# Attention scores of batches 1 to 14 from scaled fp16 parts of x2 instead of fp32r parts

## The chip, the cores and the metric

The kernel runs on one core of a Trainium2 chip. Its engines are TensorE (PE in the profile, with its weight loads shown apart as PEld), VectorE (DVE), ScalarE (ACT), GpSimd (POOL) and SyncE (SP, which issues most DMAs). The metric is the device time of one execution in microseconds. Before the change it is 1338.56 us, the median of 3 runs (1338.45 to 1338.69).

## The reference, cut to what matters

Sixteen batches of x, each 512 tokens by 512 features, go through two residual steps. fc1 is 2048 x 512, fc2 384 x 2048, and each batch adds a 128 x 2048 expert that its index picks.

```
h      = gelu(x @ fc1_w.T + fc1_b)                      # 512 x 2048 per batch
x      = x + concat(h @ fc2_w.T + fc2_b, h @ experts_w[i].T + experts_b[i])     # called x2 below
scores = tanh(x @ W1 + b1) @ v                          # W1 is 512 x 128, one score per token
p      = softmax(scores under a prefix, suffix or "not itself" mask)
out    = x + (p @ x) / number of unmasked tokens
```

The change is about `x @ W1`, the product that the tanh reads, in batches 1 to 14.

## The kernel before, in words

Everything lies transposed: features on the 128 partitions, tokens along the free side, so x of a batch is four chunks `chunk(b, c)` of 128 x 512 in `xr`. Each engine has its program written out by hand; there is no scheduler. An engine works its program strictly from first to last, and where it needs another's result it waits on a semaphore (`e.wait_ge`).

The large products run in fp16 in two parts. A value times a power of two is rounded to fp16 (the high part, made by ACT: `hh`, `xh`, `eh`), the rest is taken as fp16 again (the low part, made by DVE: `hl`, `xl`, `el`, line 1176), and three matmuls add high x high, high x low and low x high. fc1 uses seven products per pair of hidden tiles in place of eight: `product1` to `product7` in `cycle`. Between them ACT copies a half bank of PSUM (`copy_first`, `copy_fifth`, line 701) and DVE adds two halves (`add_first`, line 1225, and `add_second`, line 1230). `product7` of a pair waits for that pair's `add_first` (semaphore `added0`).

One batch b goes through these stages on PE. Six cycles of fc1, fc2 for output chunk 0 among the last of them, then fc2 for chunks 1 and 2. In the middle of chunk 1 stands `chain_sum`, a small matmul (line 342) that sums the bounds of batch b+1 over the partitions; DVE turns them into powers of two at once (`batch_scales`, lines 1134 to 1148). fc2 for chunk 3 follows, and then `opening(b)`: the attention products of chunks 0, 1 and 2 (`attend`, lines 484 to 487), the end of fc2 for chunk 3, products 1, 5, 6, 2 of pair 0 and product 1 of pair 1 of batch b+1, `attend(b, 3)`, and right behind it `product7(b+1, 0)`.

The product with W1 is made of three fp32r matmuls per chunk: `awl` x `x2h`, `awh` x `x2h`, `awh` x `x2l`. ACT rounds the chunk to fp32r (`split_x2_high`), DVE subtracts to get the rest (`x2_low`, line 1236). Chunk 3 comes late: ACT evacuates it from PSUM (`evacuate(b, 3)`, line 826) in the opening itself.

DVE does four kinds of work: low parts, the PSUM additions, the scales, and the pooling (scans and products over tokens, lines 1328 to 1454) of the batch before. The pooling is a Python generator, and `pool(n)` puts its next n instructions in at that place, so it fills DVE's time between the pieces that PE waits for. Between `batch_scales(b+1)` and `add_first(b+1, 0)` DVE has in this order: four `combine`, three pool steps, `x2_low(b, 0)`, low parts of x for batch b+1 with pool steps among them, `x2_low(b, 1)`, more of the same, `x2_low(b, 2)` and nine pool steps.

In batch 0 there is a lead-in of its own. DVE makes the masks (`masks`, 13 small instructions on 128 x 16) before the low parts of fc2's third weight chunk.

Of the kernel before, what the change touches and what calls it, by code (L numbers as in the profile page):

```python
# [35 lines left out]
def build(nc, xT, idx, pt, w1, b1, w2, b2, ew, eb, aw, ab, av, iota, ident, tokens, out):  # L36
# [14 lines left out]
    def over(name, shape, at, dt=f32):  # L51
# [18 lines left out]
    x2h_at = (here(), g_at, g_at + 8 * S)  # L70
    x2h = [nc.alloc_sbuf_tensor_at(f"x2h{c}", [P, S], f32r, offset=at) for c, at in enumerate(x2h_at)]
# [9 lines left out]
    awl = [sb("awl0", [P, A], f32r), sb("awl1", [P, A], f32r),  # L81
           nc.alloc_sbuf_tensor_at("awl2", [P, A], f32r, offset=early_at)]
    awh = nc.alloc_sbuf_tensor_at("awh", [P, KD, A], f32r, offset=aws_at)
    x2l_at = (here(), g_at + 4 * S, g_at + 12 * S)
    x2l = [nc.alloc_sbuf_tensor_at(f"x2l{c}", [P, S], f32r, offset=at) for c, at in enumerate(x2l_at)]
# [144 lines left out]
    def sems(name, n):  # L230
# [5 lines left out]
    vcol_in, vmax_done, v_scaled, atth_done, attl_done = (  # L236
        sem(n) for n in ("vcolin", "vmax", "vscaled", "atth", "attl"))
# [96 lines left out]
    def tensor_program(eng):  # L334
# [142 lines left out]
        def attend(b, c):  # L477
# [151 lines left out]
        e.wait_ge(vmax_done, 1)  # L629
        chain_sum(9, hc(1), vc + 1)  # L630
# [65 lines left out]
    def scalar_program(eng):  # L696
# [137 lines left out]

        def split_x2_high(b, c):
            e.wait_ge(x2_done, nth_chunk(b, c))
            if c in (1, 2):
                e.wait_ge(xl_done, nth_x(b + 1, (T1, T3)[c - 1]))
            copy(x2h[c][:, :], chunk(b, c)).then_inc(x2h_done)

        def tanh(b):
# [6 lines left out]
            act(att, pa, ACT.Tanh, bias=abs_[:, 0:1]).then_inc(tanh_done)  # L848
# [122 lines left out]
        for b in range(1, B):  # L971
# [138 lines left out]
    def vector_program(eng):  # L1110
# [39 lines left out]
        def batch_scales(b):  # L1150
            chain_scale(8 + b, hc(b), hc(b) + 3 if b > 1 else vc + 1)
# [754 lines left out]
```

## Time and profile before

| what | value |
|---|---|
| median of 3 runs | 1338.56 us |
| the profiled execution's own time | 1338.24 us |
| its span | 1336.5 us |
| one batch in steady state (rows of one place, batch 5 to 6) | 81.4 us |
| PE busy | 1329.4 us, 99% |
| DVE busy | 1246.9 us, 93% |
| ACT busy | 877.9 us, 66% |
| granted clock of TensorE | full (1.00), the 2.4 GHz level, in every slice |

The span runs from the first to the last instruction; 1.7 us of the execution lie outside it. Matmuls are pipelined: one shows as longer than the distance to the next, so the distance between starts is what it costs PE. DVE and ACT show a similar overlap of some 0.09 us between an instruction and the next.

### The profile page before, as it was taken

What the parts mean: (1) busy time and instruction counts of PE and PEld (TensorE: products, weight loads), DVE (VectorE), ACT (ScalarE), POOL (GpSimd) and SP (SyncE); (2) the same over time, 40 slices, a digit from 0 to 9 for tenths busy, and PEclk for the clock granted to TensorE, in tenths of its full rate; (3) what the DMA queues carried; (4) which work ended last, traced back from release to release, by engine and by line L of the source; (5) the groups of instructions that cost most, each with busy time, mean ns of one, the idle gap of its engine ahead of it and who ended that gap; (6) DMA issues with size and microseconds to landing.
All of it is one profiled execution on the core that took longest, in us unless ns stands there. A gap on an engine that the chain in (4) does not pass through costs nothing.

```text
span 1336.5 us, 21986 instructions
## 1 busy us (share of the span) xinstructions
PE 1329.4 (99%) x8681; PEld 864.5 (65%) x8681; DVE 1246.9 (93%) x2097; ACT 877.9 (66%) x1523; POOL 7.4 (1%) x12
## 2 busy tenths in 40 slices
PE   9999999999999999999999999999999999999998
PEld 4458476584856748567584765847668485674855
DVE  7988899999999999999999999999999999999998
ACT  4868848476593756938478484775847669385762
POOL 0000000000000000000000000000000000000002
PEclk9999999999999999999999999999999999999999
DMA  8410020110201102011020211102011020110006
GB/s 296 145 46 32 1 72 25 48 49 1 79 17 57 39 1 80 16 64 33 8 80 8 66 31 36 60 1 80 17 55 40 1 80 16 64 33 6 33 15 118
DMA packets 30488, 65.13 MB, mean 49 GB/s; under 512 B 6194, under 2 KB 7858, under 8 KB 27954
## 3 DMA queue, kind: packets, MB, share of 16 engines
q1 hardware_dynamic: 28802, 61.11, 14.0%
q0 software_dynamic: 1152, 2.09, 1.2%
q8 instruction: 68, 1.11, 0.4%
q10 hardware_dynamic: 432, 0.53, 0.1%
q14 instruction: 34, 0.28, 0.1%
HBM read 44.86 MB, written 18.87 MB: 48 GB/s over the span
## 4 chain that ended last, share of the span: by engine, by line
PE 99%; DMA 0%; DVE 0%; ACT 0%; issue 0%; DVEq 0%; ACTq 0%
PE ps L458 16%; PE ps L460 16%; PE ps L459 16%; PE ps L377 14%; PE ps L379 14%; PE ps L378 14%; PE ps L348 1%; PE ps L484 1%; PE ps L485 1%; PE ps L487 1%; PE ps L359 1%; PE ps L363 1%; PE ps L361 1%; PE ps L491 0%; DMA xr<-in_xT 0%; PE ps L569 0%
## 5 line engine op out<-in xcount | busy, mean ns | idle before, releaser
L460 PE MATMUL ps<-hl,w2h 128*128 128x512 f16 x768 | 291.1, 379 | 0.0
L458 PE MATMUL ps<-hh,w2l 128*128 128x512 f16 x768 | 291.1, 379 | 0.0
L459 PE MATMUL ps<-hh,w2h 128*128 128x512 f16 x768 | 291.0, 379 | 0.0
L377 PE MATMUL ps<-xh,w1h 128*128 128x256 f16 x960 | 261.7, 273 | 0.0
L378 PE MATMUL ps<-xl,w1h 128*128 128x256 f16 x960 | 261.7, 273 | 0.0
L379 PE MATMUL ps<-xh,w1l 128*128 128x256 f16 x960 | 261.7, 273 | 0.0
L726 ACT ACTIVATE g<-ps,b1s,ds 128x512 f32<-128x512 f32 x240 | 173.4, 773 | 97.6 <-PE ps L379 84.4
L377 PE MATMUL ps<-xh,ch 128*128 128x256 f16 x720 | 196.5, 273 | 0.0
L378 PE MATMUL ps<-xl,ch 128*128 128x256 f16 x720 | 196.3, 273 | 0.0
L379 PE MATMUL ps<-xh,cl 128*128 128x256 f16 x720 | 196.3, 273 | 0.0
L1176 DVE SCALAR_TENSOR_TENSOR hl<-g,ix,hh 128x512 f16<-128x512 f32 x244 | 178.4, 744 | 3.1
L701 ACT ACTIVATE hh<-g,ix 128x512 f16<-128x512 f32 x244 | 162.1, 718 | 0.0
L701 ACT ACTIVATE ps<-ps 128x256 f32<-128x256 f32 x120 | 44.6, 371 | 163.8 <-PE ps L379 163.8
L460 PEld LDWEIGHTS ps<-hl,w2h 128*128 128x128 f16 x768 | 75.1, 98 | 90.6
L458 PEld LDWEIGHTS ps<-hh,w2l 128*128 128x128 f16 x768 | 75.1, 98 | 87.4 <-DVE hl L1176 3.0
L459 PEld LDWEIGHTS ps<-hh,w2h 128*128 128x128 f16 x768 | 75.1, 98 | 82.7 <-issue 0.7
L377 PEld LDWEIGHTS ps<-xh,w1h 128*128 128x128 f16 x960 | 93.9, 98 | 19.0
L378 PEld LDWEIGHTS ps<-xl,w1h 128*128 128x128 f16 x960 | 93.9, 98 | 18.8
L379 PEld LDWEIGHTS ps<-xh,w1l 128*128 128x128 f16 x960 | 93.9, 98 | 10.8
L458 PE MATMUL ps<-hh,el 128*128 128x512 f16 x240 | 91.1, 380 | 0.0
L460 PE MATMUL ps<-hl,eh 128*128 128x512 f16 x240 | 91.0, 379 | 0.0
L459 PE MATMUL ps<-hh,eh 128*128 128x512 f16 x240 | 91.0, 379 | 0.0
(246 smaller groups left out, 2351.2 us busy)
## 6 DMA issues: line engine op xcount, KB each, us to landing
xr<-in_xT SPq DMA_DIRECT2D x62, 256.0 KB, 3.2
er<-in_ew SPq DMA_DIRECT2D x15, 1024.0 KB, 5.5
out<-xr SPq DMA_DIRECT2D x60, 256.0 KB, 2.4
raw<-in_w SPq DMA_DIRECT2D x28, 256.0 KB, 6.0
er<-in_w SPq DMA_DIRECT2D x3, 1024.0 KB, 9.9
out<-sums POOLq DMA_DIRECT2D x8, 255.5 KB, 5.2
xr<-in_ew SPq DMA_DIRECT2D x1, 1024.0 KB, 5.8
out<-xn SPq DMA_DIRECT2D x3, 256.0 KB, 3.2
```

The costliest lines, as they stand in the source:

```text
L348: m = mm(pf[k % 4], w1r[k][:, c * P:(c + 1) * P], xr[:, 0, c, :], start=c == 0, stop=c == KD - 1)
L359: mm(pf[k % 4], w1h[:, k, c, :], xh[:, c, :], start=c == 0, stop=False)
L361: mm(pf[k % 4], w1h[:, k, c, :], xl[:, c, :], start=False, stop=False)
L377: mm(to, wh, mh, start=i in (1, 5) and c == 0, stop=False, skip_group_check=True)
L378: mm(to, wh, ml, start=False, stop=False, skip_group_check=True)
L379: m = mm(to, wl, mh, start=False, stop=c == 1, skip_group_check=True)
L458: mm(po(b, o), wl, hh[:, k, :], start=False, stop=False, skip_group_check=True)
L459: mm(po(b, o), wh, hh[:, k, :], start=False, stop=False, skip_group_check=True)
L460: m = mm(po(b, o), wh, hl[:, k, :], start=False, stop=k == NH - 1, skip_group_check=True)
L701: return act(o, x, ACT.Copy, scale=scale)
L726: act(in_two(g_of(b, k)), src, ACT.Gelu, bias=b1s[:, k:k + 1], scale=ds1[:, b % 2, p:p + 1]).then_inc(gelu_done)
L1176: return stt(o, src, scale, hi, ALU.mult, ALU.subtract)
```

## The change

ACT now first multiplies a chunk by a per-batch scale and writes it as fp32 (`scale_x2` into `x2s`), and then rounds that times 2^-11 to fp16 (`x2h`). DVE's `x2_low` makes the low part from the two as fp16, 2^11 times as large as it would be (`x2l = x2s - 2^11 * x2h`). W1 is kept as three fp16 tiles, `awh`, `awl` and `awd`, the last `awh` times 2^-11. The three matmuls per chunk stay, in fp16. For chunk 3 ACT does only `scale_x2`, and DVE makes the high part too. The tanh undoes the scale (`x2_back`). The scale comes from a bound on x2 that `x2_bound` works out on DVE for batches 1 to 14 at the end of `batch_scales`. Three fixed columns (v, W1, the biases) get their maxima in batch 0 in `static_columns`; a small DMA brings the expert biases for it. The masks move later in batch 0, behind `sums_low(2)`. In `opening`, DVE's `x2_low(b, 3)` now stands ahead of `add_first(b+1, 0)`, and one pool step moves from between them and `add_second` to the end.

```diff
@@ tensor_program
             if 0 < b < LAST:
-                e.wait_ge(awh_done, 1)
-                e.wait_ge(x2h_done, nth_split(b, c))
-                mm(pa, awl[c][:, :], x2h[c][:, :], start=start, stop=False)
+                e.wait_ge(aw_high, 2)
+                if c < 3:
+                    e.wait_ge(x2h_done, 3 * (b - 1) + c + 1)
+                else:
+                    e.wait_ge(x3_high, b)
+                mm(pa, awl[:, c, :], x2h[c][:, :], start=start, stop=False)
                 mm(pa, awh[:, c, :], x2h[c][:, :], start=False, stop=False)
                 e.wait_ge(x2l_done, nth_split(b, c))
-                mm(pa, awh[:, c, :], x2l[c % 3][:, :], start=False, stop=stop).then_inc(attended)
+                mm(pa, awd[:, c, :], x2l[c][:, :], start=False, stop=stop).then_inc(attended)
@@ scalar_program
+        def scale_x2(b, c):
+            e.wait_ge(x2_done, nth_chunk(b, c))
+            e.wait_ge(x2_step, 5 * b)
+            if c in (1, 2):
+                e.wait_ge(xl_done, nth_x(b + 1, (T2, T4)[c - 1]))
+            copy(x2s[c][:, :], chunk(b, c), x2_scale[:, b % 2:b % 2 + 1]).then_inc(x2_scaled)
+
         def split_x2_high(b, c):
-            e.wait_ge(x2_done, nth_chunk(b, c))
-            if c in (1, 2):
-                e.wait_ge(xl_done, nth_x(b + 1, (T1, T3)[c - 1]))
-            copy(x2h[c][:, :], chunk(b, c)).then_inc(x2h_done)
+            scale_x2(b, c)
+            e.wait_ge(x2_scaled, nth_split(b, c))
+            copy(x2h[c][:, :], x2s[c][:, :], 2.0 ** -11).then_inc(x2h_done)
...
             evacuate(b, 3)
+            if b:
+                scale_x2(b, 3)
             copy_fifth(n, 0)
-            if b:
-                split_x2_high(b, 3)
...
-                for c in range(KD):
-                    copy(awl[c][:, :], aws[:, c, :]).then_inc(awl_high)
-                e.wait_ge(awl_low, KD)
-                copy(awh[:, :, :], aws[:, :, :]).then_inc(awh_done)
+                e.wait_ge(ix_done, 9)
+                copy(awh[:, :, :], aws[:, :, :], scale_of(ac)).then_inc(aw_high)
+                e.wait_ge(awl_low, 1)
+                copy(awd[:, :, :], awh[:, :, :], 2.0 ** -11).then_inc(aw_high)
@@ vector_program, batch_scales
+            if b == 1:
+                e.wait_ge(ex_done, 9)
+                eng.tensor_reduce(x2_tmp[:, 1:2], ex[:, w2c:w2c + 3], AX.X, ALU.max).then_inc(vmax_done)
+                e.wait_ge(vmax_done, 6)
+                ts(w2_all, x2_tmp[:, 1:2], 2.0 ** 18, None, ALU.mult).then_inc(vmax_done)
+                e.wait_ge(vmax_done, 7)
+            if b < LAST:
+                x2_bound(b)
+
+        def x2_bound(b):
+            t, u, done, i = x2_tmp[:, 0:1], x2_tmp[:, 1:2], 5 * (b - 1), slice(b % 2, b % 2 + 1)
+            e.wait_ge(x2_step, done)
+            ts(t, ex[:, ec(b):ec(b) + 1], 2.0 ** 20, w2_all, ALU.mult, ALU.max).then_inc(x2_step)
+            e.wait_ge(x2_step, done + 1)
+            stt(u, t, ex[:, hc(b):hc(b) + 1], ex[:, xc(b):xc(b) + 1], ALU.mult, ALU.max).then_inc(x2_step)
+            e.wait_ge(x2_step, done + 2)
+            ts(t, u, ex[:, bc:bc + 1], 2.0 ** -10, ALU.max, ALU.mult).then_inc(x2_step)
+            e.wait_ge(x2_step, done + 3)
+            eng.reciprocal(x2_scale[:, i], t).then_inc(x2_step)
+            ts(x2_back[:, i], t, ex[:, ac:ac + 1], 2.0 ** 11, ALU.mult, ALU.mult).then_inc(x2_step)
@@ vector_program, x2_low
-            e.wait_ge(x2h_done, nth_split(b, c))
-            if c == 3:
-                e.wait_ge(attended, nth_chunk(b, 0))
-            tt(x2l[c % 3][:, :], chunk(b, c), x2h[c][:, :].bitcast(f32), ALU.subtract).then_inc(x2l_done)
+            if c < 3:
+                e.wait_ge(x2h_done, 3 * (b - 1) + c + 1)
+            else:
+                e.wait_ge(x2_scaled, nth_split(b, c))
+                ts(x2h[c][:, :], x2s[c][:, :], 2.0 ** -11, None, ALU.mult).then_inc(x3_high)
+                e.wait_ge(x3_high, b)
+            stt(x2l[c][:, :], x2h[c][:, :], -2.0 ** 11, x2s[c][:, :], ALU.mult, ALU.add).then_inc(x2l_done)
@@ vector_program, batch 0
         column(w2c + 2, er[:, 0, :]).then_inc(big_done)
+        static_columns()
         chain_scale(8, w2c + 2, w2c + 3)
...
         w1_low(3)
-        masks()
...
         sums_low(2)
+        masks()
         add_first(1, 0)
@@ vector_program, end of the loop over batches
+            x2_low(b, 3)
             add_first(b + 1, 0)
-            x2_low(b, 3)
-            pool(2)
+            pool(1)
             add_second(b + 1, 0)
             attention_low(b)
             add_first(b + 1, 1)
-            pool(2)
+            pool(3)
```

What stands in DVE's program at the end of `batch_scales` of a batch in the loop (`ex`, `ix`, `ds`, `is` are the scales, `lift` holds x2's own, `g` is the first `combine`), before the change:

```order
L1134 SCALAR_TENSOR_TENSOR ex<-ps,lift 128x3
L1137 TENSOR_SCALAR ex<-ex 128x3
L1139 RECIPROCAL ix<-ex 128x3
L1143 TENSOR_SCALAR ds<-ex 128x8
L1147 TENSOR_SCALAR ds<-ex 128x1
L1148 TENSOR_SCALAR is<-ix 128x1
L1147 TENSOR_SCALAR ds<-ex 128x3
L1148 TENSOR_SCALAR is<-ix 128x3
L1219 TENSOR_TENSOR g<-xr 128x512
```

and after it:

```order
L1158 TENSOR_SCALAR ds<-ex 128x3
L1159 TENSOR_SCALAR is<-ix 128x3
L1179 TENSOR_SCALAR lift<-ex,lift 128x1
L1181 SCALAR_TENSOR_TENSOR lift<-lift,ex 128x1
L1183 TENSOR_SCALAR lift<-lift,ex 128x1
L1185 RECIPROCAL lift<-lift 128x1
L1186 TENSOR_SCALAR lift<-lift,ex 128x1
L1251 TENSOR_TENSOR g<-xr 128x512
```

Five small instructions stand between the scales and the first `combine`; everything behind them, up to `add_first(b+1, 0)`, keeps its order.

DVE's program in the opening of a batch in the loop, before (L1236 is `x2_low(b, 3)`, L1225 `add_first(b+1, 0)`, L1230 `add_second(b+1, 0)`, L1401 to L1418 are pool steps):

```order
L1401 SCALAR_TENSOR_TENSOR raw<-raw 128x512
L1225 TENSOR_TENSOR ps<-ps,fifth 128x256
L1236 TENSOR_TENSOR x2l_67<-xr,x2h_71 128x512
L1404 SCALAR_TENSOR_TENSOR raw<-raw 128x512
L1412 SCALAR_TENSOR_TENSOR xr<-raw,xr 128x512
L1230 TENSOR_TENSOR ps<-ps,fifth 128x256
L1176 SCALAR_TENSOR_TENSOR hl<-raw,cols,hh 128x512
L1225 TENSOR_TENSOR ps<-ps,fifth 128x256
L1415 TENSOR_TENSOR raw<-raw 128x511
```

and after (L1270 and L1272 are `x2_low(b, 3)`, L1257 `add_first`, L1262 `add_second`, L1438 and L1441 the scans):

```order
L1438 SCALAR_TENSOR_TENSOR raw<-raw 128x512
L1270 TENSOR_SCALAR x2h_71<-x2s_66 128x512
L1272 SCALAR_TENSOR_TENSOR x2l_75<-x2h_71,x2s_66 128x512
L1257 TENSOR_TENSOR ps<-ps,fifth 128x256
L1441 SCALAR_TENSOR_TENSOR raw<-raw 128x512
L1262 TENSOR_TENSOR ps<-ps,fifth 128x256
L1208 SCALAR_TENSOR_TENSOR hl<-raw,cols,hh 128x512
L1257 TENSOR_TENSOR ps<-ps,fifth 128x256
L1449 SCALAR_TENSOR_TENSOR xr<-raw,xr 128x512
```

The addition that `product7(b+1, 0)` waits for now has two DVE instructions of chunk 3 ahead of it, and the pool step of line 1412 (1449 now) stands behind the next `add_first`.

## Rows read from the trace of the kernel before

**Rows 1.** The page: busy time by engine, and the chain that ended last by engine.
```profile
PE 1329.4 (99%) x8681; PEld 864.5 (65%) x8681; DVE 1246.9 (93%) x2097; ACT 877.9 (66%) x1523; POOL 7.4 (1%) x12
...
PE 99%; DMA 0%; DVE 0%; ACT 0%; issue 0%; DVEq 0%; ACTq 0%
```

**Rows 2.** Timeline of PE, fc2, then the end of chunks 0 to 2's attention: start, duration us.
```profile
560.02 0.38 PE L458 MATMUL ps<-hh,w2l 128*128 128x512 f16 x1
...
561.10 0.38 PE L460 MATMUL ps<-hl,w2h 128*128 128x512 f16 x1
...
579.23 0.38 PE L460 MATMUL ps<-hl,eh 128*128 128x512 f16 x1
...
581.54 0.39 PE L458 MATMUL ps<-hh,el 128*128 128x512 f16 x1
```

**Rows 3.** The same view, attention of batch 6, chunk 3, then product7(7, 0).
```profile
587.30 0.27 PE L379 MATMUL ps<-xh,w1l 128*128 128x256 f16 x1
...
588.12 0.28 PE L377 MATMUL ps<-xh,ch 128*128 128x256 f16 x1
```

**Rows 4.** Timeline of DVE, batch_scales(7) in batch 6; in brackets idle time and releaser.
```profile
556.32 0.16 DVE L1134 SCALAR_TENSOR_TENSOR ex<-ps,lift 128x3 f32<-128x3 f32 x1 [0.43 <-PE ps L342]
556.52 0.17 DVE L1137 TENSOR_SCALAR ex<-ex 128x3 int32<-128x3 int32 x1
...
557.45 0.22 DVE L1148 TENSOR_SCALAR is<-ix 128x3 f32<-128x3 f32 x1
557.58 0.69 DVE L1219 TENSOR_TENSOR g<-xr 128x512 f32<-128x512 f32 x1
```

**Rows 5.** Timeline of DVE, opening of batch 6.
```profile
584.82 1.22 DVE L1401 TENSOR_TENSOR_SCAN raw<-raw 128x512 f32<-128x512 f32 x1
586.30 0.43 DVE L1225 TENSOR_TENSOR ps<-ps,fifth 128x256 f32<-128x256 f32 x1 [0.27 <-PE ps L379]
586.64 0.68 DVE L1236 TENSOR_TENSOR x2l<-xr,x2h 128x512 fp32r<-128x512 f32 x1
587.24 1.22 DVE L1404 TENSOR_TENSOR_SCAN raw<-raw 128x512 f32<-128x512 f32 x1
```

**Rows 6.** Timeline of ACT, opening of batch 6.
```profile
584.99 0.78 ACT L826 ACTIVATE xr<-ps,ebs,ds 128x512 f32<-128x512 f32 x1 [1.58 <-PE ps L460]
```

**Rows 7.** DVE's groups by line and shape: busy us, mean ns | idle before.
```profile
L1343 DVE TENSOR_SCALAR raw<-raw,cF 128x512 f32<-128x512 f32 x15 | 7.2, 482 | 0.0
L1412 DVE SCALAR_TENSOR_TENSOR xr<-raw,xr 128x512 f32<-128x512 f32 x60 | 40.6, 676 | 0.0
L1176 DVE SCALAR_TENSOR_TENSOR hl<-g,ix,hh 128x512 f16<-128x512 f32 x244 | 178.4, 744 | 3.1
```

**Rows 8.** ACT's groups by line and shape, the same columns.
```profile
L701 ACT ACTIVATE hh<-g,ix 128x512 f16<-128x512 f32 x244 | 162.1, 718 | 0.0
```

**Rows 9.** Timeline of DVE and PEld where PE waited for DVE, batch 2.
```profile
223.21 1.40 DVE L1176 SCALAR_TENSOR_TENSOR hl<-g,ix,hh 128x512 f16<-128x512 f32 x2
...
224.67 0.10 PEld L458 LDWEIGHTS ps<-hh,w2l 128*128 128x128 f16 x1 [0.33 <-DVE hl L1176]
```

**Rows 10.** Timeline of DVE and PE, end of batch 0's lead-in.
```profile
69.77 0.17 DVE L1276 CAST early<-pts 128x16 f32<-128x16 int32 x1
71.44 2.73 DVE L1176 SCALAR_TENSOR_TENSOR w2l<-er,ix,w2h 128x512 f16<-128x512 f32 x4
...
97.47 0.43 DVE L1225 TENSOR_TENSOR ps<-ps,fifth 128x256 f32<-128x256 f32 x1 [2.53 <-PE ps L379]
99.44 0.27 PE L377 MATMUL ps<-xh,ch 128*128 128x256 f16 x1
```

**Rows 11.** Timeline of batch 1: a rest of DVE, the opening's first add, product7(2, 0).
```profile
153.43 1.23 DVE L1365 TENSOR_TENSOR_SCAN raw<-raw 128x512 f32<-128x512 f32 x1 [0.34 <-ACT raw L864]
...
179.28 0.41 DVE L1225 TENSOR_TENSOR ps<-ps,fifth 128x256 f32<-128x256 f32 x1
181.00 0.28 PE L377 MATMUL ps<-xh,ch 128*128 128x256 f16 x1
```

More of the change, by code:

```diff
@@ L69, in build @@
     g = sb("g", [P, GR, S])
-    x2h_at = (here(), g_at, g_at + 8 * S)
-    x2h = [nc.alloc_sbuf_tensor_at(f"x2h{c}", [P, S], f32r, offset=at) for c, at in enumerate(x2h_at)]
+    x2_at = [here(), g_at, g_at + 8 * S]
     fifth = sb("fifth", [P, 2, HALF])
@@ L80, in build @@
     early = sb("early", [P, A])
[L81 to L85, printed above, removed]
+    awh = sb("awh", [P, KD, A], f16)
+    awd = nc.alloc_sbuf_tensor_at("awd", [P, KD, A], f16, offset=aws_at)
+    x2s_at = (here(), g_at + 4 * S, g_at + 12 * S, here())
+    x2s = [nc.alloc_sbuf_tensor_at(f"x2s{c}", [P, S], f32, offset=at) for c, at in enumerate(x2s_at)]
     raw_at = here()
@@ L94, in build @@
     zF, zB = mF, mB
-    awl.append(nc.alloc_sbuf_tensor_at("awl3", [P, A], f32r, offset=raw_at + 4 * (2 * S + 2 * 516)))
-    x2h.append(nc.alloc_sbuf_tensor_at("x2h3", [P, S], f32r, offset=raw_at + 4 * 15 * S))
-    rows_at = 2 * S + 2 * 516 + A
+    rows_at = 2 * S + 2 * 516
+    awl = nc.alloc_sbuf_tensor_at("awl", [P, KD, A], f16, offset=raw_at + 4 * (rows_at + 10 * S))
+    x2_at.append(raw_at + 4 * 15 * S)
+    x2h, x2l = ([nc.alloc_sbuf_tensor_at(f"{n}{c}", [P, S], f16, offset=at + skip) for c, at in enumerate(x2_at)]
+                for n, skip in (("x2h", 0), ("x2l", 2 * S)))
     row = [raw[:, rows_at + i * S:rows_at + (i + 1) * S] for i in range(7)]
@@ L235, in build @@
         sem(n) for n in ("e0in", "idxin", "ptin", "b1in", "b2in", "awin", "abin", "avin", "ioin", "eyein", "lcolin"))
[L236 to L237 removed]
+    vcol_in, vmax_done, v_scaled, atth_done, attl_done, x2_step, x2_scaled, x3_high = (
+        sem(n) for n in ("vcolin", "vmax", "vscaled", "atth", "attl", "x2step", "x2scaled", "x3h"))
     (bits_set, summed, tile_done, p1, p5, p6, p7, p3, fc2_done, half_done, attended, score_done, nat_done, cols_done,
@@ L244, in build @@
     (gelu_done, hh_done, x0h_done, w1h_done, w2h_done, eh_done, xh_done, first_copied, fifth_copied, seeded, x2_done,
-     x2_half, squared, x2h_done, tanh_done, scored, exp_running, exp_done, awl_high, awh_done, ones_high, three_high,
+     x2_half, squared, x2h_done, tanh_done, scored, exp_running, exp_done, aw_high, ones_high, three_high,
      inverted, seen, cleared, xn_done, own_done, scol_done, part_done, own_p_done, block_w_done, sums_kept) = (sem(n) for n in (
          "gelu", "hh", "x0h", "w1h", "w2h", "eh", "xh", "first", "fifth", "seed", "x2", "x2half", "sq", "x2h", "tanh",
-         "scored", "exprun", "exp", "awlh", "awh", "sumone", "sumthree", "inv", "seen", "cleared", "xn", "own", "scol", "part", "ownp",
+         "scored", "exprun", "exp", "awh", "sumone", "sumthree", "inv", "seen", "cleared", "xn", "own", "scol", "part", "ownp",
          "bw", "kept"))
@@ L628, in tensor_program @@
         e.wait_ge(bound_step, 6)
-        e.wait_ge(vmax_done, 1)
-        chain_sum(9, hc(1), vc + 1)
+        e.wait_ge(vmax_done, 5)
+        chain_sum(9, hc(1), NC)
         fc2(0, 2, range(8, 16))
@@ L847, in tanh @@
                 e.wait_ge(sums_low_done, 2)
-            act(att, pa, ACT.Tanh, bias=abs_[:, 0:1]).then_inc(tanh_done)
+            act(att, pa, ACT.Tanh, bias=abs_[:, 0:1], scale=x2_back[:, b % 2:b % 2 + 1] if b else 1.0).then_inc(tanh_done)
             e.wait_ge(tanh_done, b + 1)
@@ L1150, in batch_scales @@
         def batch_scales(b):
-            chain_scale(8 + b, hc(b), hc(b) + 3 if b > 1 else vc + 1)
+            chain_scale(8 + b, hc(b), hc(b) + 3 if b > 1 else NC)
             fc1_scale(b, 8 + b, 0, PAIRS)
@@ L1455, in pooling, with static_columns @@
                 yield
+        def static_columns():
+            e.wait_ge(vcol_in, 16)
+            column(vc, vcol[:, :]).then_inc(vmax_done)
+            e.wait_ge(aw_in, 16)
+            column(ac, aws[:, :, :].rearrange("p a b -> p (a b)")).then_inc(vmax_done)
+            e.wait_ge(b2_in, 32)
+            column(bc, b2s[:, :]).then_inc(vmax_done)
+            biggest(x2_tmp[0:E, 0:1], fifth[0:E, 0, 0:P]).then_inc(vmax_done)
+            e.wait_ge(vmax_done, 4)
+            tt(mx[0:E, bc:bc + 1], mx[0:E, bc:bc + 1], x2_tmp[0:E, 0:1], ALU.max).then_inc(vmax_done)
         pools = itertools.chain.from_iterable(pooling(b) for b in range(LAST))
@@ L1468, in vector_program @@
         eng.memset(ones16[:, :], 1.0).then_inc(ones_set)
-        for lo, hi, power in ((0, 2, -14), (2, 11, -12), (11, 16, -14), (16, 18, -12)):
+        for lo, hi, power in ((0, 2, -14), (2, 11, -12), (11, 16, -14), (16, 20, -12)):
             eng.memset(lift[:, lo:hi], 2.0 ** power).then_inc(ones_set)
@@ L1552, in vector_program @@
         weight_sums_first(0)
-        e.wait_ge(vcol_in, 16)
-        column(vc, vcol[:, :]).then_inc(vmax_done)
         bounds(1)
@@ L1621, in vector_program @@
             if b == 1:
-                for c in range(KD):
-                    e.wait_ge(awl_high, c + 1)
-                    tt(awl[c][:, :], aws[:, c, :], awl[c][:, :].bitcast(f32), ALU.subtract).then_inc(awl_low)
+                e.wait_ge(aw_high, 1)
+                low_part(awl[:, :, :], aws[:, :, :], scale_of(ac), awh[:, :, :]).then_inc(awl_low)
             pool(3 if b == 1 else 4)
```

11 lines of the change are left out of this document (6 added, 5 removed).

## The prediction

> **What bounds the kernel now.** I read the page first: PE is busy for 99% of the span and the chain that ended last is 99% PE [rows 1]. The table of waits has PE waiting only at the start and in the tail, so in the loop it is the distance between matmul starts that makes the time. But DVE is busy for 93% [rows 1], which is an average. I then looked for the stretch in which DVE never rests. In each batch DVE waits for the small matmul `chain_sum` (0.43 us idle at 556.32, the first of [rows 4]) and next rests at the first `add_first` of the opening, at 586.30, for 0.27 us [rows 5]. In the 29.5 us between there is nothing but work. PE takes the result of that `add_first` (end 586.73) at 588.12 [rows 3, 5], 1.39 us later. Latency from DVE's end to PE is small: where PE does wait for DVE, the second `hl` ends at 224.61 and the weight load starts at 224.67 [rows 9]; its matmul starts with it. So DVE has at most 1.39 - 0.06 = 1.33 us to spare in that stretch. The change puts work exactly there. The timelines of batches 2 to 14 show the same; batch 1 differs a little: the add ends at 179.69, PE takes it at 181.00, and DVE had no rest before it [rows 11].
>
> **The change, part by part.**
>
> PE. An fp16 matmul over 512 columns costs 0.216 us (five distances from 560.02 to 561.10) [rows 2]. The nine fp32r ones of chunks 0 to 2 begin 0.216 after 579.23 and end at 581.54, 2.09 us or 0.233 each [rows 2]; in fp16 1.94. The three of chunk 3 take from 587.30 + 0.11 (the length of a 256-column step) to 588.12, 0.71 us [rows 3], against 0.65. Together 0.20 us per batch, 14 batches, 2.8 us less, if nobody is late.
>
> ACT, chunks 0 to 2. Two copies instead of one. A scaled copy costs about 0.62 us behind another (0.718 less the overlap) [rows 8], so some 2 us per batch more on an engine 66% busy [rows 1]. It rests for 1.58 us right before `evacuate(b, 3)` [rows 6] and longer before. `scale_x2` of chunks 1 and 2 also waits for a later low part (T2, T4 instead of T1, T3), which moves them by one or two DVE instructions. I cost this at nothing: PE takes these chunks after 579.2, and DVE, which reads `x2h` too, is about 1 us later itself. Without that cover it would be an ACT copy, 0.6 us, on PE's path.
>
> DVE, `x2_bound`. Five small instructions between the scales and the first `combine`. A small instruction that waits for the one ahead starts 0.20 us after it when it lasts 0.16 to 0.17 (556.32 to 556.52), that is its duration plus 0.04; one that doesn't wait starts 0.13 us after (557.45 to 557.58) with 0.22 [rows 4]. The new ones with a pointer scalar last 0.21 to 0.22 as those do. The first starts where `combine` used to; then three dependent steps of 0.25, the reciprocal's 0.09 to the unchained last one, and 0.13 to `combine`: 0.75 + 0.09 + 0.13 = 0.97 us. Bounds: 0.65 (five times 0.13) and 1.25 (five times 0.25).
>
> The Trainium skill says otherwise of the waits: in "VectorE: DVE Perf Modes", section "The DRAIN you can't avoid", eight copies with a semaphore after each took as long as eight with one at the end, "the semaphore costs nothing extra here". [Rows 4] do not agree for instructions this small: 0.20 with a wait, 0.13 without, although the one with the wait is the shorter. By that rule the sum of this part would be 0.65 us, the low bound above.
>
> DVE, `x2_low` of chunks 0 to 2. The subtraction (0.68, 0.60 from start to start) [rows 5] becomes a scalar_tensor_tensor with a constant. The nearest row with a constant scalar, line 1412, has 0.676 [rows 7]: no difference. The one with a pointer scalar and fp16 out has 0.744 [rows 7]; that is the upper bound, +0.07 for each of four.
>
> DVE, chunk 3. A tensor_scalar over 512 columns makes the high part. Line 1343 takes 0.482 with a pointer scalar [rows 7]; a constant saves the 0.05 between 0.22 and 0.17 [rows 4]: 0.43. Bounds 0.30 (an estimate: of 0.482 all but 0.22 is the columns' share, halved for an output of half the bytes, and 0.17 for the rest) and 0.68 (the rate of line 1412). The low part depends on it (+0.04), and both now stand ahead of `add_first`.
>
> The opening then comes out so, in batch 6's times. DVE could start its next instruction at 586.03 - 0.09 = 585.94 [rows 5]. With 0.97 more it is there at 586.91. ACT's scaled chunk is there before: the evacuation ends at 585.77 [rows 6], the copy 0.03 + 0.72 later, 586.52. High part 586.91 to 587.34; low part from 587.38; `add_first` 0.60 later at 587.98 to 588.41; `product7` at 588.47. It was 588.12. So PE comes out of the opening 0.35 us later than before, where the cheaper matmuls alone would have brought it there 0.20 us earlier. DVE's anchor for the next batch is again a PE instruction, so this is the growth of the period.
>
> What is late next. One scan stands between this `add_first` and `add_second`, as before minus one step; the step is made up after the second `add_first`, so by the pair 2 addition DVE is 0.0 to 0.1 us behind where it was, relative to PE, and later rests absorb that. I find no second wait.
>
> Batches. `x2_bound` for batch b+1 stands in batches 0 to 13, the chunk 3 work in 1 to 14. Batches 2 to 13: 12 x 0.35 = 4.2. Batch 1: DVE rests 0.34 us for ACT in between, which hides that much of the 0.97; 0.63 + 0.47 + 0.60 (what now stands ahead of the add) against a margin of 1.31 - 0.06 [rows 11]: +0.45. Batch 14: no `x2_bound`; DVE starts when ACT's copy is there, 586.56, and `product7` is at 588.12 again: 0. Batch 0: `static_columns` and `x2_bound(1)` add about 2.7 us to DVE (a 512-column maximum 0.6, eleven small ones), `masks` moves 1.67 us (69.77 to 71.44) past the low parts; at its end DVE rests 2.53 us and the add's margin is then still 99.44 - 97.90 [rows 10]. Of the 2.7, about 1.4 stand behind `chain_scale(9)`; 1.4 + 1.67 = 3.1 against 2.53 + 1.48: 0. Without that cover it would be at most 1 us once. The additional DMA (8 KB) is in a queue that is quiet by then: 0.
>
> Sum: 4.2 + 0.45 + 0 = +4.7 us on the profiled execution's 1338.24 us (span 1336.5 and 1.7 outside), so 1342.9; the median of the runs stood 0.3 above, 1343.3.
>
> **The rivals.**
>
> 1. All of DVE's new work is hidden and PE gets its 2.8 us: 1335.8. For it: PE bounds 99% of the chain [rows 1]. Against it: the new work ahead of the add is 0.97 + 0.47 + 0.60 = 2.04 us, and there is 0.27 of rest plus 1.33 of margin less the 0.20 that PE arrives earlier, 1.40. It needs 0.64 us of estimates to be wrong at once.
>
> 2. Waits between the small instructions cost nothing, 0.65 in place of 0.97: +0.03 per batch in 2 to 13, 0.2 in batch 1, so +0.6: 1339.2, no change. This is the case that goes with the skill's rule; [rows 4] speak against it.
>
> 3. `x2_low` runs at the slower form's rate, 0.07 us in four places: +0.28 in 13 batches, +3.6 us: 1346.9. For it: fp16 out, as in the 0.744 rows [rows 7]. Against it: the constant scalar of line 1412. With the tensor_scalar at the full 0.68 another 0.25 x 14 = 3.5: 1350.4.
>
> 4. DVE reaches the opening in time, and ACT's copy decides in every batch as it does in batch 14: it ends at 586.52, and high part, low part and add behind it bring `product7` to 588.12 as before. The gain on PE is then waited away, and the time stays at 1338.6 within 0.7. It decides where DVE's new work ahead of the opening is under 0.62 us (586.56 - 585.94).
>
> **How the numbers follow.** Chances: my forecast with its own spread (1341.3 to 1345) 0.58; rival 3 in part or whole 0.18; rivals 2 and 4 0.15; rival 1 0.09. The predicted time is the forecast's, 1343.3. The range leaves out rival 1, part of the no-change cases and the far end of rival 3: 1338.8 to 1348.5. A difference of 0.2%, 2.7 us, is what a measurement of this kernel can tell from none, and 1341.3 lies 2.7 above the median before. Slower: 0.58 x 0.9 + 0.18 = 0.70; faster 0.06, since rival 1 at 1335.8 is only just past 0.2%; same 0.24.
>
> **What would show it.** The mean distance of `attend`'s matmuls in chunks 0 to 2 should be 0.216. PE should have one new wait per batch, of 0.4 to 0.6 us, before `product7` of pair 0 for DVE's `add_first`, and a part of it before the third matmul of chunk 3 for `x2l`. The five `x2_bound` instructions should take 0.97 us from the first's start to `combine`, and DVE should have no rest at the first `add_first`. The period should be 81.75 us rather than 81.4. The prediction is wrong if PE shows no wait there, if DVE rests before the opening, or if a stall shows at pair 1 or 2 or in batch 0 that I took as covered.

## The result, and the profile after

The changed kernel takes 1343.56 us (median of 7 runs, 1343.11 to 1343.85) against 1338.52 (7 runs on the same chip, 1338.41 to 1338.69): a ratio of 1.0038, 95% interval 1.0028 to 1.0047. It is slower by 5.0 us where 4.7 were forecast. The profiled execution took 1343.56 with a span of 1341.8 us.

The page of the kernel after, busy time and the chain that ended last by engine; it answers to [rows 1]:

```profile
PE 1333.0 (99%) x8681; PEld 850.9 (63%) x8681; DVE 1261.1 (94%) x2184; ACT 915.3 (68%) x1562; POOL 7.4 (1%) x12
...
PE 68%; DVE 31%; issue 0%; ACT 0%; DVEq 0%
```

The shares of busy time hardly moved. The chain did: 99% of it was PE, and now 31% is DVE. That is not because PE is idle for long. In each batch of the loop a handover from DVE to PE is now the last to arrive, and from there the chain follows DVE back without a gap to the anchor, DVE's first instruction behind `chain_sum`. In batch 6 the profile lets the chain cross at chunk 3's low part (to the matmul at 590.40 below) and not at the addition, since it names no releaser for `product7`'s weight load. That `product7` waits for the addition is read from the times below and from the experiments.

DVE of the kernel after, end of `batch_scales(7)` in batch 6 (start, duration, in brackets idle time and releaser), against [rows 4]:

```profile
558.62 0.16 DVE L1145 SCALAR_TENSOR_TENSOR ex<-ps,lift 128x3 f32<-128x3 f32 x1 [0.43 <-PE ps L346]
...
559.88 0.21 DVE L1179 TENSOR_SCALAR lift<-ex,lift 128x1 f32<-128x1 f32 x1
560.13 0.22 DVE L1181 SCALAR_TENSOR_TENSOR lift<-lift,ex 128x1 f32<-128x1 f32 x1
...
560.63 0.17 DVE L1185 RECIPROCAL lift<-lift 128x1 f32<-128x1 f32 x1
560.71 0.20 DVE L1186 TENSOR_SCALAR lift<-lift,ex 128x1 f32<-128x1 f32 x1
560.84 0.69 DVE L1251 TENSOR_TENSOR g<-xr 128x512 f32<-128x512 f32 x1
```

From 559.88, where `combine` used to come, to 560.84 are 0.96 us: three dependent steps of 0.25, then 0.08 to the instruction that does not depend on the reciprocal, then 0.13.

The same timeline at the opening of batch 6, against [rows 5]:

```profile
589.21 0.40 DVE L1270 TENSOR_SCALAR x2h<-x2s 128x512 f16<-128x512 f32 x1
589.65 0.69 DVE L1272 SCALAR_TENSOR_TENSOR x2l<-x2h,x2s 128x512 f16<-128x512 f16 x1
590.26 0.42 DVE L1257 TENSOR_TENSOR ps<-ps,fifth 128x256 f32<-128x256 f32 x1
```

No instruction has a bracket: the rest of 0.27 us is gone. PE's weight loads at the same place show who releases them:

```profile
589.67 0.10 PEld L491 LDWEIGHTS ps<-x2h,awl 128*128 128x128 f16 x1 [0.23 <-DVE x2h L1270]
...
590.39 0.10 PEld L494 LDWEIGHTS ps<-x2l,awd 128*128 128x128 f16 x1 [0.61 <-DVE x2l L1272]
590.80 0.10 PEld L381 LDWEIGHTS ps<-xh,ch 128*128 128x128 f16 x1 [0.31 <-issue]
```

These brackets are idle time of the weight loads, which start ahead of their matmuls, and not what PE loses; and "issue" says nothing of the addition, for in the kernel before the same load has an idle time of 0.28 <-issue although the addition had ended 1.38 us earlier. What PE loses is read from its matmuls, against [rows 2, 3]. First those from chunk 0's first to the one behind chunk 2, then the last 256-column matmul ahead of chunk 3, chunk 3 and `product7(7, 0)`:

```profile
581.75 0.38 PE L491 MATMUL ps<-x2h,awl 128*128 128x512 f16 x1
...
583.69 0.38 PE L462 MATMUL ps<-hh,el 128*128 128x512 f16 x1
...
589.44 0.27 PE L383 MATMUL ps<-xh,w1l 128*128 128x256 f16 x1
589.67 0.39 PE L491 MATMUL ps<-x2h,awl 128*128 128x512 f16 x1
589.90 0.38 PE L492 MATMUL ps<-x2h,awh 128*128 128x512 f16 x1
590.40 0.39 PE L494 MATMUL ps<-x2l,awd 128*128 128x512 f16 x1
590.83 0.27 PE L381 MATMUL ps<-xh,ch 128*128 128x256 f16 x1
```

The nine matmuls of chunks 0 to 2 now take 583.69 - 581.75 = 1.94 us, as forecast, 0.15 less than before. Then PE stands still three times within 1.4 us. From 589.44 to 589.67 are 0.23 us where such a step takes 0.11, so 0.12 is lost for the high part. From 589.90 to 590.40 are 0.50 where an fp16 matmul takes 0.22: 0.28 for the low part. From 590.40 to 590.83 are 0.43: 0.21 for the addition. Together that is 0.61 us, the fp16 form gives back 0.15 + 0.06 = 0.21, and the difference, 0.40, is what a batch grew by. The table of waits has the idle time of the weight loads for the first two, in 13 and 14 batches (us in all, times, longest):

```profile
PEld ps L494 <- DVE x2l L1272: 8.2, 14, 0.6
...
PEld ps L491 <- DVE x2h L1270: 2.8, 13, 0.2
```

For the period I take the matmul `chain_sum` of the scales (three columns, bf16), which occurs once per batch from 2 to 14. This row gives its count, the first and the last start, before and after:

```profile
L342 PE MATMUL ps<-mx,oneb x13: 167/168/168, 230.5 to 1207.3; 128*128 128x3 bf16 x13
```
```profile
L346 PE MATMUL ps<-mx,oneb x13: 167/168/168, 231.2 to 1212.8; 128*128 128x3 bf16 x13
```

Twelve periods are 976.8 us before and 981.6 after: 81.40 and 81.80 us, +0.40 per batch. Every experiment below is read by this number (in experiments 4 and 6 over eleven periods), since start and tail of the program differ by some tenths between kernels.

### The profile page after: what moved, and what is told of

Same layout as the page of the kernel before. It is cut to its first block, busy times and chain, and to the rows that moved or that the text cites. A ratio compares the mean times of both kernels' runs of the same rounds, so it can differ in the third digit from the quotient of the medians.

```text
span 1341.8 us, 22098 instructions
## 1 busy us (share of the span) xinstructions
PE 1333.0 (99%) x8681; PEld 850.9 (63%) x8681; DVE 1261.1 (94%) x2184; ACT 915.3 (68%) x1562; POOL 7.4 (1%) x12
## 4 chain that ended last, share of the span: by engine, by line
PE 68%; DVE 31%; issue 0%; ACT 0%; DVEq 0%
PE ps L381 13%; PE ps L382 13%; PE ps L383 13%; PE ps L462 8%; PE ps L464 8%; PE ps L463 8%; DVE xl L1208 4%; DVE raw L1477 3%; DVE g L1251 3%; DVE x2l L1272 2%; DVE raw L1438 2%; DVE raw L1481 2%; DVE raw L1435 1%; DVE raw L1432 1%; DVE raw L1402 1%; DVE raw L1441 1%
```

## The experiments

The theory, T: the time is the delay of one addition. DVE runs from `chain_sum` to `add_first(b+1, 0)` without a rest, the change puts 2.0 us more ahead of it than its slack, and `product7(b+1, 0)` comes later by the excess. The rivals: W, that the waits between `x2_bound`'s small instructions cost nothing and something else is late; L, that the new form of the low parts is slow wherever it stands; M, that the move of the masks in batch 0 has a part in it.

**1. The bound at another place.** Nothing is left out; `x2_bound(b)` is issued where DVE has slack, after the batch's last `add_second` (in batch 2 at the start of cycle 4).

```diff
-            if b < LAST:
-                x2_bound(b)
...
             add_second(b, PAIRS - 1)
+            if b < LAST and b != 2:
+                x2_bound(b)
```

> The changed kernel, with x2_bound(b) moved out of the end of batch_scales to where DVE waits for ACT's expert split (behind add_second of the last pair; in batch 2, which has places() there, into the cycles). Theory (DVE's unbroken stretch from the scales to the opening's add sets the period, and x2_bound is 0.97 us of it): every batch now looks as batch 14 did in the changed kernel, product7 0.08 us earlier against the kernel before than without the change, because ACT's scaled copy of chunk 3 (586.52 in batch 6's old times) is what the chain copy, high, low, add then starts from: 14 x 0.08 = 1.1 us under the kernel before, about 1337.5. Rival 1 (the cost is in chunk 3's chain alone, ACT copy to DVE to PE, and x2_bound is hidden): no change from 1343.6. Rival 2 (the four low parts at a slower rate are what is lost): 1342 or more.

Measured: 1337.55 us (10 runs) against 1338.61 before on that chip, ratio 0.9993 (0.9983 to 1.0002); period 81.33. Taking five instructions of 0.2 us out of one stretch brings back 6 us. Against the kernel before it is not shown to be faster, for the interval includes 1. The first of the five for batch 7 now comes here; the stretch of batch 6 starts some 65 us earlier, with `combine` at 557.11 right behind the scales:

```profile
622.23 0.20 DVE L1177 TENSOR_SCALAR lift<-ex,lift 128x1 f32<-128x1 f32 x1
```

DVE and PEld at the opening of batch 6:

```profile
585.93 0.43 DVE L1268 TENSOR_SCALAR x2h<-x2s 128x512 f16<-128x512 f32 x1 [0.36 <-ACT x2s L708]
586.39 0.69 DVE L1270 SCALAR_TENSOR_TENSOR x2l<-x2h,x2s 128x512 f16<-128x512 f16 x1
```
```profile
587.14 0.10 PEld L494 LDWEIGHTS ps<-x2l,awd 128*128 128x128 f16 x1 [0.25 <-DVE x2l L1270]
```

DVE is there early and rests 0.36 us for ACT's scaled chunk. That is the prediction's rival 4: ACT's copy decides, and the cheaper matmuls are waited away but for 0.07 us per batch (the rival had 1338.6, no gain at all, because it left ACT's copy at its old time). L is refuted as the main cause: all low parts are still in the new form, and the kernel is no slower than before.

**2. The bound moved, and the old order in the opening.** On top of experiment 1 the addition goes ahead of chunk 3's parts again.

```diff
-            x2_low(b, 3)
             add_first(b + 1, 0)
-            pool(1)
+            x2_low(b, 3)
+            pool(2)
             add_second(b + 1, 0)
             attention_low(b)
             add_first(b + 1, 1)
-            pool(3)
+            pool(2)
```

> As e1, and in the opening add_first(b+1, 0) stands ahead of x2_low(b, 3) again, with two pool steps behind as before the change. Theory: DVE is at the add in time (586.30), the high part follows at 586.64 to 587.04, before PE wants it at 587.35, the low part ends at 587.8 where PE wants it at 587.78. PE then gets what its fp16 matmuls save, 0.20 us in 14 batches: 1338.5 - 2.8 = 1335.7, with up to 0.05 a batch lost at the low part: 1335.7 to 1336.5. Rival (chunk 3's path through DVE costs what the matmuls save, whatever the order): 1337.5 to 1338.5 as in e1.

Measured: 1343.93 us (5 runs), ratio 1.0042 (1.0028 to 1.0055), period 81.80. A clear miss by 8 us. DVE and ACT of this kernel, opening of batch 6:

```profile
588.67 0.43 DVE L1255 TENSOR_TENSOR ps<-ps,fifth 128x256 f32<-128x256 f32 x1 [0.71 <-ACT fifth L708]
589.01 0.42 DVE L1268 TENSOR_SCALAR x2h<-x2s 128x512 f16<-128x512 f32 x1
```
```profile
587.58 0.72 ACT L708 ACTIVATE x2s<-xr,lift 128x512 f32<-128x512 f32 x1
588.21 0.36 ACT L708 ACTIVATE fifth<-ps 128x256 f32<-128x256 f32 x1
```

The addition reads `fifth`, and ACT makes `fifth` behind the scaled chunk: the change had swapped those two copies on ACT. So the addition cannot come before `x2s` is done, whatever DVE's order says, and DVE rests 0.71 us for it with the two parts of chunk 3 still to make. In the kernel after this second swap is harmless, because there DVE wants `x2s` first. The two orders belong together, and I had undone one.

**3. The old order alone.** The edit of experiment 2 without that of experiment 1; ACT's order stays as changed.

```diff
-            x2_low(b, 3)
             add_first(b + 1, 0)
-            pool(1)
+            x2_low(b, 3)
+            pool(2)
...
-            pool(3)
+            pool(2)
```

> The changed kernel with only the opening's order put back: add_first ahead of x2_low(b, 3), x2_bound stays at the end of batch_scales. Theory: DVE comes to the opening 0.97 us late (586.9 in batch 6's old times), add 0.34, high part 587.26 to 587.66, low part 587.7 to 588.38, third matmul at 588.44, product7 0.22 behind at 588.66 against 588.53 in the changed kernel: 0.13 more in 13 batches, 1345.3. Rival (the order of the two is what costs the changed kernel its time, since product7 waits for the add): under 1343.6, toward 1338.

Measured: 1345.79 us (4 runs), ratio 1.0055 (1.0039 to 1.0070), period 81.94. The number is met; PE's weight loads of this kernel show the place:

```profile
590.71 0.10 PEld L491 LDWEIGHTS ps<-x2h,awl 128*128 128x128 f16 x1 [0.56 <-DVE x2h L1270]
...
591.44 0.10 PEld L494 LDWEIGHTS ps<-x2l,awd 128*128 128x128 f16 x1 [0.61 <-DVE x2l L1272]
591.51 0.10 PEld L381 LDWEIGHTS ps<-xh,ch 128*128 128x128 f16 x1
```

`product7`'s load follows chunk 3's last one at once: here it is not the addition that is late but the two parts of chunk 3. The change's order in the opening was the better one given what stands ahead of it. The old order on both engines with the bound in place was not run, but ACT's order is not what costs here: its `fifth` ends at 589.65 and the addition starts at 589.93, as soon as the scan ahead of it lets it.

**4. The bound's chain twice.** The same five instructions with the same dependences on scratch values, behind `x2_bound`; they are extra work and change no result.

```diff
             batch_scales(b + 1)
+            if b + 1 < LAST:
+                spare_chain(b + 1)
```

> The changed kernel with a copy of x2_bound's five instructions (same kinds, same waits, on spare columns) behind it in 13 batches. Theory: the stretch has no slack left, so their 0.97 us are paid in full: 13 x 0.97 = 12.6, 1356.1. Rival 1 (DVE is not what bounds the period): up to 1345. Rival 2 (a wait on the instruction ahead costs nothing, so that the five take 0.65): 1352.

Measured: 1355.75 us (one run, before 1338.61), period 82.75, +0.94 per batch over the kernel after. DVE has no slack there any more, and every tenth that is put in front of the addition is paid in full.

**5. The same chain in the kernel before.** `spare_chain` as in experiment 4, in the kernel before, which has nothing else of the change.

```diff
+        def spare_chain(b):
+            t, u, c, done = spare[:, 0:1], spare[:, 1:2], spare[:, 4:5], 1 + 5 * (b - 2)
+            e.wait_ge(vmax_done, done)
+            ts(t, c, 1.0, spare[:, 5:6], ALU.mult, ALU.max).then_inc(vmax_done)
+            e.wait_ge(vmax_done, done + 1)
+            stt(u, t, spare[:, 5:6], spare[:, 6:7], ALU.mult, ALU.max).then_inc(vmax_done)
...
             batch_scales(b + 1)
+            if b + 1 < LAST:
+                spare_chain(b + 1)
```

> The kernel before the change with the five spare instructions, chained by waits as in x2_bound, at the end of batch_scales in 13 batches. Theory: DVE has 0.27 us of rest and 1.33 us of margin in front of the opening's add, so 0.97 us cost nothing there: 1338.5, product7 unmoved, the add ending 0.7 us later. Rival (work put there is paid in any kernel): 1351.

Measured: 1341.53 us (one run, before 1338.44), period 81.60, +0.20 per batch where I had expected none. DVE, PEld and PE of this kernel, the anchor and the opening of batch 6:

```profile
557.85 0.16 DVE L1135 SCALAR_TENSOR_TENSOR ex<-ps,lift 128x3 f32<-128x3 f32 x1 [0.43 <-PE ps L343]
...
588.44 0.41 DVE L1238 TENSOR_TENSOR ps<-ps,fifth 128x256 f32<-128x256 f32 x1
588.75 0.68 DVE L1249 TENSOR_TENSOR x2l<-xr,x2h 128x512 fp32r<-128x512 f32 x1
```
```profile
589.49 0.19 PEld L488 LDWEIGHTS ps<-x2l,awh 128*128 128x128 f32 x1 [0.34 <-DVE x2l L1249]
```
```profile
589.49 0.50 PE L488 MATMUL ps<-x2l,awh 128*128 128x512 f32 x1
589.84 0.28 PE L378 MATMUL ps<-xh,ch 128*128 128x256 f16 x1
```

PE waits for chunk 3's low part, not for the addition. The addition had 1.33 us to spare, but the low part stands one instruction behind it and PE takes it one matmul before `product7`: it ends at 586.64 + 0.68 = 587.32 [rows 5], and the third matmul of chunk 3 starts at 587.88 (588.12 less one matmul of 0.24) [rows 3], a margin of 0.56 - 0.06 = 0.50. Ahead of that DVE could start 0.36 us before it did (585.94, as the prediction has it, against 586.30), so 0.97 should make the low part 0.97 - 0.36 - 0.50 = 0.11 late. The third matmul starts 589.49 - 557.85 = 31.64 us behind the anchor where it was 31.56, 0.08 late. The other 0.11 us of the 0.20 lie between this matmul and `product7`: 0.35 where they were 0.24. Its weight load of 0.19 us now starts with it and not, as before, 0.23 ahead of it; that this is the cause is likely and not tested. I had read the slack from one consumer only.

**6. Five small instructions without dependences.** As experiment 4, but the five only read a constant column.

```diff
-            e.wait_ge(vmax_done, done)
-            ts(t, c, 1.0, spare[:, 5:6], ALU.mult, ALU.max).then_inc(vmax_done)
-            e.wait_ge(vmax_done, done + 1)
...
+            for i in range(5):
+                ts(spare[:, i:i + 1], c, c, None, ALU.mult).then_inc(vmax_done)
```

> The changed kernel with five more small instructions at the end of batch_scales (a pointer scalar, 128x1) that do not wait for each other, in 13 batches. Theory: 0.13 us each from start to start, paid in full, 13 x 0.65 = 8.5: 1352.0. With e4 it gives the price of a wait on the instruction ahead: 12.6 - 8.5 = 4.1 us. Rival (the waits cost nothing): as e4.

Measured: 1351.08 us (one run, before 1338.44), period 82.39, +0.59 per batch over the kernel after, 0.118 for each. DVE of this kernel, the five in one row with the `combine` behind them:

```profile
563.43 0.69 DVE L1192 TENSOR_SCALAR spare<-spare 128x1 f32<-128x1 f32 x5
564.03 0.68 DVE L1257 TENSOR_TENSOR g<-xr 128x512 f32<-128x512 f32 x1
```

0.60 us from first start to `combine`, where the chained five take 0.94 to 0.96. The waits alone are thus about 0.35 us per batch of the bound's 0.96, and W is refuted. (The two sets differ in kind too, since the unchained ones are all tensor_scalar, but one instruction lasts about 0.2 us in both.) The Trainium skill, "VectorE: DVE Perf Modes", section "The DRAIN you can't avoid", has a semaphore after each of eight copies cost nothing; for these 128x1 instructions no run here agrees with that, since dependent ones start 0.25 us apart and independent ones 0.12.

**7. The masks where they were.** `masks()` goes back behind `w1_low(3)`; all else as in the kernel after.

```diff
         w1_low(3)
+        masks()
...
         sums_low(2)
-        masks()
         add_first(1, 0)
```

> The changed kernel with masks() back at its old place in batch 0. Theory: batch 0 has cover either way; 1343.6 within 0.3, and product7(1, 0) where it was. Rival (the masks behind sums_low(2) cost or save time in batch 0): a shift of product7(1, 0) by up to 1.7 us.

Measured: 1343.83 us (one run, before 1338.44), period 81.82. First matmul of `product7(1, 0)`, the kernel after and this one:

```profile
99.71 0.27 PE L381 MATMUL ps<-xh,ch 128*128 128x256 f16 x1
```
```profile
99.67 0.27 PE L381 MATMUL ps<-xh,ch 128*128 128x256 f16 x1
```

Before it was at 99.44 [rows 10]. Between the two that differ in the masks alone are 0.04 us, so M has no part in the growth of the period and next to none in batch 0.

**8. The high part of chunk 3 on ACT.** On top of experiment 1, to shorten DVE's stretch by 0.43 us.

```diff
             if b:
-                scale_x2(b, 3)
+                split_x2_high(b, 3)
             copy_fifth(n, 0)
@@ x2_low
-            if c < 3:
-                e.wait_ge(x2h_done, 3 * (b - 1) + c + 1)
-            else:
-                e.wait_ge(x2_scaled, nth_split(b, c))
-                ts(x2h[c][:, :], x2s[c][:, :], 2.0 ** -11, None, ALU.mult).then_inc(x3_high)
-                e.wait_ge(x3_high, b)
+            e.wait_ge(x2h_done, nth_split(b, c))
```

> As e1, but ACT makes the high part of chunk 3 too (scale, then round, as for the other chunks) and DVE only the low part, still ahead of the add. Theory: ACT's second copy ends at 587.17 in batch 6's old times (PE wants it at 587.35), DVE's low part runs 587.21 to 587.89, the add 587.81 to 588.24, product7 at 588.38: 0.26 us a batch later than before the change, 14 x 0.26 = 3.6, 1342.1. Rival (a DVE instruction less must be faster): under e1's time.

Measured: 1340.22 us (10 runs) against 1338.44, ratio 1.0013 (1.0004 to 1.0023), period 81.53. Slower than experiment 1 by 0.20 per batch, which is the direction forecast. Against the kernel before it is +0.13 where I had 0.26, since I had counted from the old times of ACT's copy, and PE now lets it start 0.14 us earlier. DVE of this kernel:

```profile
587.51 0.69 DVE L1262 SCALAR_TENSOR_TENSOR x2l<-x2h,x2s 128x512 f16<-128x512 f16 x1 [1.03 <-ACT x2h L705]
```

DVE has a full microsecond to rest and the kernel is slower: in the opening the latency of the chain evacuation, scaled chunk, high part, low part counts, and ACT's 0.63 for the high part is longer than DVE's 0.43.

**9. The bound moved, the old order on DVE, and the old order on ACT.** Experiment 2 with ACT's two copies swapped back too.

```diff
+            copy_fifth(n, 0)
             if b:
                 scale_x2(b, 3)
-            copy_fifth(n, 0)
```

> As e2 (x2_bound moved, add_first ahead of x2_low(b, 3)), and on ACT copy_fifth stands ahead of scale_x2(b, 3) again, as it did before the change. Theory: e2 lost its time because DVE's add waited for ACT's copy_fifth, which the scaled copy had been put in front of (DVE idle 0.71 us there in e2); with it back the add starts when PE's product is there, the high part at 586.56 in batch 6's old times, the low part ends at 587.70, the third matmul starts 0.06 late, product7 at 587.98 against 588.12: 14 x 0.14 = 2.0 us under the kernel before, 1336.5. Rival (DVE's two instructions for chunk 3 cost the gain in any order): 1338 or more.

Measured: 1336.82 us (11 runs, 1336.44 to 1337.33) against 1338.48, ratio 0.9988 (0.9979 to 0.9997), period 81.25. It beats both kernels and confirms the reading of experiment 2: one swap of two ACT copies is worth 7 us there. DVE, ACT and PE of this kernel, opening of batch 6:

```profile
586.01 0.43 DVE L1255 TENSOR_TENSOR ps<-ps,fifth 128x256 f32<-128x256 f32 x1
...
586.86 0.69 DVE L1270 SCALAR_TENSOR_TENSOR x2l<-x2h,x2s 128x512 f16<-128x512 f16 x1
```
```profile
585.38 0.37 ACT L708 ACTIVATE fifth<-ps 128x256 f32<-128x256 f32 x1
585.64 0.72 ACT L708 ACTIVATE x2s<-xr,lift 128x512 f32<-128x512 f32 x1
```
```profile
587.61 0.39 PE L494 MATMUL ps<-x2l,awd 128*128 128x512 f16 x1
587.84 0.27 PE L381 MATMUL ps<-xh,ch 128*128 128x256 f16 x1
```

The addition fills the time in which ACT makes `x2s`, and no rest of DVE is listed there. Of the 0.20 us per batch that fp16 gives on PE, 0.15 comes through; the low part ends at 587.55 and PE takes it at 587.61, so the rest is a last wait for it.

**10. The chain in the kernel before, with the low part first.** Experiment 5 with the order `x2_low(b, 3)`, `add_first(b+1, 0)`, `pool(1)`, and `pool(3)` at the end.

```diff
+            x2_low(b, 3)
             add_first(b + 1, 0)
-            x2_low(b, 3)
-            pool(2)
+            pool(1)
             add_second(b + 1, 0)
             attention_low(b)
             add_first(b + 1, 1)
-            pool(2)
+            pool(3)
```

> As e5 (the kernel before with five spare instructions), and in the opening x2_low(b, 3) stands ahead of add_first, with the pool steps as in the change. Theory: e5 lost 0.20 us a batch although the add had margin, because the low part behind it had only 0.50 us (0.56 less the 0.06 of latency) against 0.97 - 0.27 = 0.70. With the low part first it ends at 587.60 and the add at 587.95, before PE wants them at 587.82 and 588.06: no loss, 1338.5. Rival (the 0.20 is the price of the spare instructions as such): 1341.5.

Measured: 1338.64 us (one run) against 1338.48, period 81.41. DVE of this kernel, opening of batch 6:

```profile
587.17 0.67 DVE L1249 TENSOR_TENSOR x2l<-xr,x2h 128x512 fp32r<-128x512 f32 x1
587.75 0.42 DVE L1238 TENSOR_TENSOR ps<-ps,fifth 128x256 f32<-128x256 f32 x1
```

With the low part ahead of the addition the same 0.97 us costs 0.01 per batch. That settles the miss of experiment 5: both results must be in time, and the two consumers want them in this order. Theory T has to name the low part beside the addition: the addition decides last in the change's order, the low part in the old one (experiments 3 and 5).

## Why the prediction was right

By its own steps, each against what was measured:

- **PE's matmuls**: 1.94 us for the nine, as forecast. Of the three of chunk 3 two wait for DVE.
- **ACT, chunks 0 to 2, at nothing**: the two groups of copies cost 0.72 and 0.63 us each, and `x2s` waits 67.9 us in all for the later low parts (rows below), yet PE shows no wait for chunks 0 to 2. Right.
- **`x2_bound`**: 0.97 forecast, 0.96 measured; experiments 4 and 6 give 0.94 for it by itself, and 0.59 without its dependences. The low bound, 0.65, is what five without waits were to cost: experiment 6 has 0.59.
- **Low parts**: 0.666 mean for the new form against 0.676 taken from line 1412. Rival 3 is out.
- **High part of chunk 3**: 0.402 mean, 0.44 with the dependence, for 0.43 + 0.04. Right within 0.03.
- **The opening**: the addition started 590.26 - 558.62 = 31.64 us behind the anchor; the prediction has 587.98 - 556.32 = 31.66. So DVE's half of the sum was right to 0.02.
- **The handover**: the addition ended at 590.68, `product7`'s weight load began at 590.80 and the matmul at 590.83, 0.15 behind, where I had put 0.06 from [rows 9]. This is the one term of the sum that was too small, by 0.09; the addition itself ended 0.03 earlier than forecast, so the growth is 0.40 and not 0.35, in 12 batches 0.6 us. It is a constant: `product7` begins 0.15 us behind the addition's end in all 14 batches of the kernel after, of experiment 1 and of experiment 8, while chunk 3's low part is taken 0.06 behind its end in batches 1 to 13 of the kernel after. The addition writes PSUM and the low part doesn't; whether that makes the difference is not tested.
- **Who waits**: I had looked for one new wait of 0.4 to 0.6 us before `product7`, with a part of it before the third matmul. The total is right, 0.61, but only 0.21 of it stands before `product7`; 0.28 stands before the third matmul and 0.12 before the first. The sum did not notice, because it followed DVE to the addition and all three waits come from the same late DVE.
- **Batches 1, 14, 0**: +0.43, -0.08 and +0.27 against +0.45, 0 and 0. In batch 14 PE's earlier arrival (0.14) carries ACT's copy with it, which I had left at its old time. Batch 0's 0.27 is no loss of the change's work there: it is there from the program's first 7 us, where the weight load that waits for x's transfer starts at 7.05 and started at 6.79 before. DVE still rests 0.44 us before the addition, where it rested 2.53 [rows 10].
- **Rival 1's price**: it was said to need 0.64 us of wrong estimates, from a rest of 0.27 us. The opening's own sum starts DVE at 585.94, 0.36 before 586.30, so it was 0.55.

The groups of ACT and DVE by line and shape on which this rests (busy us, mean ns, idle before and its releaser), and DVE's addition at the end of batch 0, the kernel after:

```profile
L1272 DVE SCALAR_TENSOR_TENSOR x2l<-x2h,x2s 128x512 f16<-128x512 f16 x56 | 37.3, 666 | 0.5
L1270 DVE TENSOR_SCALAR x2h<-x2s 128x512 f16<-128x512 f32 x14 | 5.6, 402 | 0.4 <-ACT x2s L708 0.4
```
```profile
L708 ACT ACTIVATE x2s<-xr,lift 128x512 f32<-128x512 f32 x56 | 40.4, 722 | 69.8 <-DVE xl L1208 67.9
L708 ACT ACTIVATE x2h<-x2s 128x512 f16<-128x512 f32 x42 | 26.5, 630 | 1.3
```
```profile
97.74 0.43 DVE L1257 TENSOR_TENSOR ps<-ps,fifth 128x256 f32<-128x256 f32 x1 [0.44 <-PE ps L383]
```

By these terms the profiled execution should have been 1342.9 and was 1343.56, 0.7 more; the median missed by only 0.3, since before's median lay 0.3 above its profiled run and after's does not. So the mechanism was right, one term of the sum, the last handover, was 0.06 where 0.15 was measured, and part of the closeness of the last figure is luck.

What the prediction did not see, though its sum did not need it, is that the change was two orders that hang together (DVE's in the opening and ACT's swap), and that the low part of chunk 3 has a smaller margin than the addition. Rival 1, everything hidden, is not reached by any of the ten kernels. Experiment 9 comes nearest, at 1336.8 against its 1335.8.

## What to carry to other kernels

An instruction that costs 0.2 us costs nothing or everything by its place: look for the stretch in which the nearly busy engine never rests, and keep bookkeeping out of it, since the same five instructions were worth 6 us there and nothing that the time shows at another place of the same batch. Read the slack of such a stretch at every result that leaves it, and not only at the last, and when an order is undone, undo it on every engine whose instructions were swapped with it. A faster matmul gives only what the latency of the chain that feeds it lets through.

## What the runs showed of the hardware

- A dependence between two 128x1 instructions on the same engine, DVE, costs about 0.12 us: 0.25 from start to start with it and 0.12 without (experiments 4 and 6). I had 0.04 on top of the duration for it, which comes to the same.
- The 128x512 tensor_scalar from fp32 to fp16 with a constant takes 0.40 to 0.43 us on DVE, against 0.63 us for the same copy on ACT and 0.67 for a scalar_tensor_tensor.
- ACT's copy with a pointer scale takes 0.72 us, the one with a constant 0.63.
- `product7`'s matmul came 0.15 us behind the end of the addition it waited for, in all 14 batches of three kernels (the one after, experiments 1 and 8), against the 0.06 that other handovers from DVE to PE show ([rows 9], and chunk 3's low part here).
- An fp32r matmul of 512 columns whose weight load had to wait for DVE took 0.35 us to the next matmul in place of 0.24 (experiment 5); an fp16 one took 0.23 in place of 0.22 (591.44 to 591.67 in experiment 3). The weight loads last 0.19 and 0.10 us.
